# Attention over two key tiles at a time: a pair of steps in one run of full-width tiles, maxima tiles ahead of score tiles

## What is computed

```python
q, k, v = xn @ Wq, xn @ Wk, xn @ Wv            # 16 heads of 32
scores = einsum('bthd,bshd->bhts', q, k) * tril(ones((T, T)))
attn = softmax(scores / T ** 0.5, axis=-1)
s = einsum('bhts,bshd->bthd', attn, v) @ Wo
g = silu(layernorm(xn) @ ternary(W).T + bias)
out = x + s * g
```

## Time and profile before

| | |
|---|---|
| three runs | 1656.3, 1650.23, 1652.95 us, median 1652.95 |
| profiled execution | 1653.39 us, its span 1651.6 us |
| TensorE busy | 1540.7 us (93%) |
| VectorE busy | 1049.1 us (64%) |
| GpSimd busy | 885.5 us (54%) |
| ScalarE busy | 770.2 us (47%) |
| mean granted clock | 0.954 |

### The profile page before, as it was taken

The page is one execution under the profiler, slowest core; times in us unless marked ns, Lnnn a source line. Parts: engine busy times, 40 slices in busy tenths (PEclk is TensorE's granted clock), DMA queues, the critical chain, the costliest instruction groups (busy, mean ns, idle before and its releaser), DMA issues.

```text
span 1651.6 us, 24364 instructions
## 1 busy us (share of the span) xinstructions
PE 1540.7 (93%) x8554; PEld 913.3 (55%) x8554; DVE 1049.1 (64%) x2357; ACT 770.2 (47%) x1614; POOL 885.5 (54%) x725
## 2 busy tenths in 40 slices
PE   6999999993999999999999999999999999799977
PEld 5788888882545445544544454444544454333755
DVE  7555445532977776776777677776777677700657
ACT  4333333320026655655665565665665565467210
POOL 4000000003027777778777776876777777768541
PEclk9999999996559999999999999999999999999988
DMA  6656556557901035045035105403603500131998
GB/s 207 194 179 194 175 181 202 179 178 181 226 27 40 21 84 142 21 90 142 22 85 113 61 28 118 114 21 84 154 21 84 142 21 14 56 113 33 291 338 300
DMA packets 109977, 201.34 MB, mean 122 GB/s; under 512 B 14368, under 2 KB 32288, under 8 KB 108832
## 3 DMA queue, kind: packets, MB, share of 16 engines
q1 hardware_dynamic: 98768, 177.79, 39.6%
q10 hardware_dynamic: 11088, 22.02, 4.1%
HBM read 123.22 MB, written 76.28 MB: 121 GB/s over the span
## 4 chain that ended last, share of the span: by engine, by line
PE 75%; DVE 10%; DMA 7%; ACT 3%; POOL 2%; issue 2%; SPq 1%; ACTq 0%; POOLq 0%; DVEq 0%
PE psP L1180 19%; PE psS L1272 16%; PE psO L1295 16%; PE psM L1247 13%; PE psL L1301 6%; DMA gr<-gate 4%; DVE mx L1053 3%; DVE psM L1050 2%; PE psL L1310 2%; ACT Pb L871 2%; PE psT L1140 2%; POOL acc L750 1%; PE psM L1272 1%; DMA Ks<-k_lo 1%; DMA Qs<-mrow 1%
## 5 line engine op out<-in xcount | busy, mean ns | idle before, releaser
L750 POOL TENSOR_TENSOR acc<-acc,Pb 128x1024 f32<-128x1024 f32 (+2 forms) x308 | 597.8, 1970 | 131.5 <-PE psO L1295 100.4
L871 ACT ACTIVATE Pb<-psS 128x512 f32<-128x512 f32 (+3 forms) x1101 | 503.0, 531 | 346.0 <-PE psS L1272 330.0
L1053 DVE TENSOR_REDUCE mx<-psM 128x1 f32<-128x512 f32 x722 | 458.8, 684 | 170.8 <-PE psM L1247 170.0
L1272 PE MATMUL psS<-Qs,Ks 97*128 97x512 f32 (+1 forms) x1223 | 468.7, 403 | 14.6 <-ACT Pb L871 7.4
L1247 PE MATMUL psM<-Ks,Qs 96*128 96x512 f32 (+3 forms) x1218 | 439.2, 395 | 34.7 <-DMA Ks<-k_lo 24.8
L1272 PEld LDWEIGHTS psS<-Qs,Ks 97*128 97x128 f32 x1223 | 227.4, 191 | 281.3 <-ACT Pb L871 115.7
L1050 DVE CUSTOM_DVE_ANT_0 psM<-psM,negm 128x128 f32<-128x128 f32 (+3 forms) x496 | 229.6, 517 | 116.4 <-PE psM L1247 115.9
L1247 PEld LDWEIGHTS psM<-Ks,Qs 96*128 96x128 f32 x1218 | 231.9, 197 | 100.4 <-DVE mx L1053 25.8
L1295 PE MATMUL psO<-Pb,Vs 128*32 128x512 f32 (+3 forms) x2304 | 272.0, 539 | 11.9 <-POOL Pb L733 11.9
L733 POOL TENSOR_SCALAR_AFFINE_SELECT Pb<-Pb 128x256 f32<-128x256 f32 x240 | 94.1, 405 | 119.5 <-ACT Pb L871 117.2
L686 POOL TENSOR_TENSOR rstd<-ve,mhalf 128x4 f32<-128x4 f32 x8 | 8.1, 1010 | 242.0 <-DVE ve L941 241.9
(11 more groups left out here) (107 smaller groups left out, 1650.7 us busy)
## 6 DMA issues: line engine op xcount, KB each, us to landing
Qs<-q_hi SPq DMA_DIRECT2D x32, 512.0 KB, 12.9
Ks<-k_hi SPq DMA_DIRECT2D x32, 512.0 KB, 11.1
xt<-in_L_attn_x SPq DMA_DIRECT2D x8, 1024.0 KB, 7.1
q_hi<-st_hi SPq DMA_DIRECT2D x32, 256.0 KB, 3.6
q_lo<-st_lo SPq DMA_DIRECT2D x32, 256.0 KB, 3.4
gate<-gs SPq DMA_DIRECT2D x32, 256.0 KB, 2.2
k_hi<-st_hi SPq DMA_DIRECT2D x32, 256.0 KB, 2.6
k_lo<-st_lo SPq DMA_DIRECT2D x32, 256.0 KB, 2.8
```

What stands on the lines that cost most here:

```text
L750: g.tensor_tensor(to[:, :, o:], to[:, :, o:], Pb[s % RING][:, heads, o:], ALU.add).then_inc(sum_done, 1)
L871: a.activation(weights(s, h)[:, o:], score_bank(s * HQ + h, last)[:, o:], ACT.Exp, scale=SCALE).then_inc(exp_done, 1)
L1053: ins = v.tensor_reduce(flat[:, heads, slots], bank[:, 0:ns * w].rearrange("p (a b c) -> p a b c", a=nh, c=w), AX.X, ALU.max)
L1272: t.matmul(score_bank(n, last)[:, o:], Ks[par][0:MROW + 1, h, j * P:(j + 1) * P], Qs[par][0:MROW + 1, h, c * CW + o:(c + 1) * CW], start=T ...
```

## The change

It has three parts. TensorE issues two steps' scores and maxima in one run, and behind it the values of both; the row sums of the chunk before stand between the two values. A head's maxima entries are issued ahead of its score tile, but for the last head of an odd slot, where they stay behind it; ScalarE's negations are moved likewise. And the planner counts the first step of chunks 1, 2 and 3 with 256 columns less.

```diff
 def step_time(s):
-    return width(s) + P
+    c, j = STEPS[s]
+    return width(s) + P - (2 * P if c and j == 0 else 0)
+
+def maxima_first(s, h):
+    return s % 2 == 0 or h < HQ - 1
...
                 for h in range(HQ):
+                    beside = max_share(qn, s - 2, h) if s >= 2 else []
+                    if maxima_first(s, h):
+                        max_rows(beside)
                     act.wait_ge(S_full, (qn * NSTEP + s) * HQ + h + 1)
                     a.activation(weights(s, h)[:, o:], score_bank(s * HQ + h, last)[:, o:], ACT.Exp, scale=SCALE).then_inc(exp_done, 1)
-                    if s >= 2:
-                        max_rows(max_share(qn, s - 2, h))
+                    if not maxima_first(s, h):
+                        max_rows(beside)
...
                     for h in range(HQ):
+                        beside = max_share(qn, slots, h) if slots is not None else []
+                        if slots is None or maxima_first(slots, h):
+                            max_scores(beside)
                         if ahead:
                             scores(*ahead, s, h, not more)
-                        if slots is not None:
-                            max_scores(max_share(qn, slots, h))
+                        if slots is not None and not maxima_first(slots, h):
+                            max_scores(beside)
...
-                for s, (c, j) in enumerate(STEPS):
+                def ahead(s):
                     if s + 2 < NSTEP:
                         run(s + 2, (qn, par), s)
                     elif s + 2 > NSTEP and more:
                         run(0, (qn + 1, 1 - par), s)
                     else:
                         run(None, None, s)
+                for gr, (c, j) in enumerate(GROUPS):
+                    s = 2 * gr
+                    ahead(s)
+                    ahead(s + 1)
                     values(s)
                     if j == 0 and (c > 0 or follows):
                         row_sums(*((qn, c - 1, not more) if c else (qn - 1, NCH - 1, False)))
+                    values(s + 1)
```

## The result

The changed kernel takes 1665.5 us (median of 4 runs, 1661.4 to 1667.6); the kernel before 1653.2 (4 runs, 1650.2 to 1656.3). The ratio is 1.0072, with a 95% interval of 1.0053 to 1.0091: slower by 12 us, where +13 was forecast. The profiled execution of the changed kernel is the fastest of its four (1661.4); of the kernel before it lies at the median (1653.4).

The account below looks back on a forecast made before the run. TensorE's order of tiles was taken to bound the kernel (93% busy). Seven quads -43 + 55 + 7 = +19, DMA waits -4, last quad -1 to 0: +14 on 1653.4, median 1666 us; range 1638 to 1683.

Parts of the forecast that it names:

- The return: TensorE's switches between full-width and 32-column tiles: one saved per pair of steps, 0.31 us, 43 us in seven quads.
- VectorE's waits: Maxima tiles wait for reductions behind three psM banks: 9.6 us a quad against 1.8 now, 55 lost in seven quads.
- plain pair: Two steps with eight full-width maxima tiles in a row: gains 0.31, pays 0.30, still takes 6.9 to 7.0 us.
- The recurrence: Earliest start of maxima tile k (from 0) behind VectorE's reductions: 1.40 + 0.60 (k - 3) us into the run.
- The sum of a quad: Saved switches, VectorE's waits and ScalarE's and GpSimd's added waits: -43 + 55 + 7 = +19 us in seven quads.
- The sign that was named: Weight loads of maxima tiles, waiting 15.1 us for plain reductions, would wait at least twice as long.
- GpSimd and ScalarE: GpSimd's additions start a run later and ScalarE's waits grow: +1.0 us a quad, 7 in seven, from 0 to 2.5.
- the last quad: The eighth quad, with almost no maxima: taken as 0, from -4 to +3 us; -1 to 0 in the sum.
- The DMA waits: TensorE's two waits (1.07 and 1.04) for the maximum's rows at step 12 go: -4 us, from 0 to -5.
- the third rival: Worse: new waits in the seven quads drop the granted clock, about 2 us a drop, 1681 us; chance 12%.
- the first rival: Faster: switches saved in full, VectorE's waits near half, 5.0 instead of 9.6 us a quad, 1632 us; chance 20%.

Follow-up runs that it names:

- the halved kernels: Kernel before and changed kernel, both with VectorE's reductions, ScalarE's exponentials and GpSimd's selects and additions over half their columns: 1591.2 and 1555.1 us.
- the even planner alone: Kernel before with a planner adding 768 columns to each step instead of 128, and maxima in front, one step at a time: 1654.9 us, ratio 1.0001.
- the mix: Changed kernel with only seven of twenty pairs two steps at a time and a planner adding 768 columns to each step: 1638.3 us, ratio 0.9918.

## Why the prediction was right

**The return.** Taken at 0.31 a pair, bounds 0.2 to 0.35. With nobody in the way 0.31 to 0.33. The prediction's own terms gave less than it took: 6.99 less 6.71 is 0.28. What they missed is in the blocks: values, row sums and values are 2.71 where 2.76 was taken (the row sums between two values take 0.86, not 0.88, and the last values 0.97, not 1.00); the run of 3.95 was right. The prediction's estimate from the Trainium skill (TensorEngine Tiling (Array Packing), Key Properties; TensorE: Matmul & The Clock Gate, Single matmul latency) was 0.33, and the halved kernels, at 0.31 to 0.33, agree with it.

**VectorE's waits.** A plain pair was to gain 0.31 and pay 0.30; it goes from 6.99 to 6.91. The recurrence had VectorE start 0.55 behind the run (0.54 in the trace) and the run 0.3 longer by its waits; it is 0.25 longer (4.20 against 3.95). It placed the largest waits in steps (6,7) and (14,15); the waits for masked tiles (L1060, up to 1.1) are there. The sum of a quad was +19/7 = 2.7; an undisturbed quad is 133.2 to 133.3 against 130.8, +2.4. The sum is better than its parts: VectorE was to cost 7.8 a quad and the others 1.0, but halving VectorE takes 4.2 out of the twenty runs of a quad (85.5 to 81.3, both at full clock), against 1.4 out of a quad of the kernel before, and halving the others as well takes out some 6 more (to 75.3). So VectorE alone accounts for about 2.8 a quad and not 7.8, and the rest of what was put down to it is held by ScalarE and GpSimd as soon as it is out of the way. The sum came out, the share of the engines did not. The edits taken apart agree in the main: scores in front are 7 us worse (0.1 a pair, as the prediction had it, would be 14 over seven quads; the later expectation had 4), and maxima in front alone do nothing. The sign that was named, loads of maxima tiles waiting at least twice as long, came (15.1 to 51.5), but it is a weak one: the even planner alone shows it too, and costs nothing.

**GpSimd and ScalarE.** Values(8) wait 0.42 to 0.46 where 0.4 was forecast, and a score tile of step 13 waits about 0.5 where 0.9 was. That eight exponentials "just fit (waits under 0.1)" was too low: the plain run with VectorE halved is 0.15 longer than with all three halved. In the last quad 0 was taken, and its part from the fifth step on went from 103.1 to 104.0.

**The DMA waits** went, as forecast, but not for the reason given. The profile has none in the stage, where before it had 2.1 us. The prediction puts this down to the planner's edit; alone that edit raised them to 3.8, and they are gone with the pairs and the old planner. The size of 4 is near: the wait of 1.07 was followed by half rate, 914.65 to 918.80 against 2.67 for the same tiles behind the wait of 1.04, so the two cost 1.07, 1.5 and 1.04, together 3.6. (The prediction took the tile of 0.63 for both; behind the second wait it is 0.40, at full rate.)

**The medians.** That +13 was forecast and +12 measured is in part luck. In the profiled executions the seven quads differ by 6.7, where +15 was forecast (+19 and -4): the one before holds half-clock stretches beyond the one behind that wait (its seven quads run from 130.8 to 134.7), and the one after holds hardly any (133.2 to 133.6). The other three executions of the changed kernel take 3.5 to 6.2 longer than the profiled one, at mean granted clocks of 0.951 and 0.952 instead of 0.955, and have no profile. So the third rival, that the new waits drop the clock, didn't come in the profiled execution, where waits of matmuls for VectorE of up to 0.8 leave the seven quads at 0.99 and 1.00, and is open for the others. In the last quad of that profile a wait of 0.81 for ScalarE was followed by half rate.

**Where the reading was too narrow.** The text named VectorE as what eats the return, and gave GpSimd and ScalarE +1.0. That gives the time of this kernel and the wrong account of what would mend it: the first rival's case (VectorE's waits at half, 1632) was run in a stronger form, VectorE halved, and the changed order still lost 4 us to the other. Behind VectorE stand ScalarE, at 0.51 an exponential against 0.47 for a score and a maxima tile and more wherever a run has fewer maxima than scores, and GpSimd's chain, of which the prediction itself said that "VectorE's waits fill the rest". A wait that hides another was counted once in the sum and forgotten in the rival.

## What to carry to other kernels

Fewer switches of an engine's mode mean longer runs of one kind, and a ring of three banks passes a longer run on to the consumer at the consumer's own pace: compare the two paces over the run, not over the stage. Work out the run length at which the first wait comes (here the weights wait from the fifth maxima tile on and the matmuls come late from the sixth), and merge only runs that stay under it; the mix did that and gained 15 us, though its planner had a part in it. When two or three engines have nearly the same pace, relieving one shows the next; an experiment that halves all of them tells whether the gain exists, and one for each of them, here done for VectorE only, tells who holds it. A weight load's wait is no price: measure the length of the run instead.

## What the runs showed of the hardware that was not expected

Blocks of 32-column tiles follow each other closely: values 0.88, row sums 0.86 and values to the next run 0.97, while each change between full-width and 32-column tiles costs about 0.1 on either side.

The same wait can cost the clock or not. 1.41 waited for GpSimd was followed in five quads of one execution by half rate, 1.6 lost in the next three blocks of the one shown, and in two quads by full rate. A wait of 0.70 to 0.73 for ScalarE at the same place of each quad, in the pairs with scores in front, was followed by half rate in three quads (135.5 each) and by full rate in four (133.9 to 134.1). In the changed kernel the waits of 0.17 to 0.30 of its weight loads, three to a plain run, left the granted clock at 1.00.
